# In the last feed-forward block of a three-block network, GpSimd issues each gather only once the preceding one has landed

## The reference

```python
def ffn(x):                       # x is the layer-normed activation, 4096 x 256
    p = sigmoid(x @ gate_w.T); p = p / p.sum(-1)
    w, idx = top_k(p, 2)          # two of 16 experts for each token
    w = w / w.sum(-1)
    gate, up = split(x @ gate_up_proj[e])      # 256 -> 2 * 128, for each expert e
    y = (silu(gate) * up) @ down_proj[e]       # 128 -> 256
    return sum over the two chosen experts of w * y
x = x + 0.5 * ffn(layernorm(x))
x = x + attention(layernorm(x))   # 16 heads of 16, causal
x = x + 0.5 * ffn(layernorm(x))
```

## Time and profile before

| | us |
|---|---|
| median of 3 runs | 785.37 |
| fastest, slowest of them | 782.91, 786.13 |
| profiled execution, first to last instruction (its span) | 862.8 |
| in it: last block, first gather issued | 593.05 |
| in it: last expert tile copied out of PSUM | 810.55 |
| in it: first and last gather behind the last store | 813.29 and 853.55 |

### The profile page before, as it was taken

The page is one execution under the profiler, slowest core; times in us unless marked ns, Lnnn a source line. Parts: engine busy times, 40 slices in busy tenths (PEclk is TensorE's granted clock), DMA queues, the critical chain, the costliest instruction groups (busy, mean ns, idle before and its releaser), DMA issues. The chain is left out here.

```text
span 862.8 us, 17915 instructions
## 1 busy us (share of the span) xinstructions
PE 666.8 (77%) x5486; PEld 538.4 (62%) x5503; DVE 520.5 (60%) x1407; ACT 403.7 (47%) x962; POOL 397.6 (46%) x466
## 2 busy tenths in 40 slices
PE   2649999978699999999999998674553999777300
PEld 1438888867367777777777776453342999666300
DVE  7887533426588888888988875378511344244333
ACT  2534666644155555556655654571112666443100
POOL 4134555555445544444554322403375554346274
PEclk9859999989699999999999999985665999889655
DMA  7873555545544434444343330051243567334453
GB/s 244 284 244 108 159 162 161 162 126 143 155 133 128 129 113 117 117 127 124 112 112 107 103 102 27 3 196 44 66 116 95 156 162 149 101 101 137 138 178 118
DMA packets 94160, 113.48 MB, mean 132 GB/s; under 512 B 11648, under 2 KB 84624, under 8 KB 94096
## 3 DMA queue, kind: packets, MB, share of 16 engines
q1 hardware_dynamic: 80240, 74.87, 27.5%
q0 software_dynamic: 13824, 37.77, 17.4%
q10 hardware_dynamic: 32, 0.02, 0.0%
HBM read 49.30 MB, written 33.55 MB: 96 GB/s over the span
## 5 line engine op out<-in xcount | busy, mean ns | idle before, releaser
L876 PE MATMUL bank<-xeT,shared 128*128 128x128 f32 x1280 | 181.2, 288 | 14.3 <-ACT xeT L992 9.1
L704 POOL DMA_INDIRECT spare<-normed,source x128 | 123.0, 961 | 140.2 <-PE bank L867 57.0
L876 PEld LDWEIGHTS bank<-xeT,shared 128*128 128x128 f32 x1280 | 166.6, 203 | 17.6 <-issue 17.3
L1142 DVE TENSOR_TENSOR hid<-bank,silu 128x128 f32<-128x128 f32 x160 | 46.6, 291 | 184.1 <-ACT silu L996 109.1
L370 POOL TENSOR_SCALAR_AFFINE_SELECT pr<-pr 128x512 f32<-128x512 f32 x128 | 81.0, 655 | 156.3 <-ACT pr L537 155.9
L883 PE MATMUL bank<-wd_sb,hid 128*128 x320 | 107.4, 419 | 47.7 <-issue 28.2
L594 DVE TENSOR_REDUCE mx<-bank 128x2 f32<-128x512 f32 (+1 forms) x192 | 127.9, 687 | 23.5 <-PE bank L443 20.9
L537 ACT ACTIVATE pr<-bank 128x512 f32<-128x512 f32 x192 | 102.8, 609 | 32.1 <-PE bank L465 19.6
L1006 ACT COPY shared<-wgu_sb 128x512 f32 x160 | 97.9, 613 | 26.0 <-DVE eid L1163 16.1
L996 ACT ACTIVATE silu<-bank 128x128 f32<-128x128 f32 x160 | 44.6, 279 | 136.6 <-PE bank L876 82.2
L715 POOL DMA_INDIRECT shared<-grouped_out,slot x64 | 62.8, 981 | 65.6 <-DVE x_sb L1316 25.1
(11 more groups left out here) (175 smaller groups left out, 1051.3 us busy)
## 6 DMA issues: line engine op xcount, KB each, us to landing
grouped_out<-shared SPq DMA_DIRECT2D x160, 128.0 KB
shared<-parts SPq DMA_DIRECT2D x154, 128.0 KB
spare<-parts SPq DMA_DIRECT2D x70, 128.0 KB
normed<-shared SPq DMA_DIRECT2D x16, 512.0 KB, 3.6
wgu_sb<-_L_ffn_gate_up_proj_dram SPq DMA_DIRECT2D x8, 512.0 KB, 8.7
out_dram<-x_sb SPq DMA_DIRECT2D x16, 256.0 KB
x_sb<-in_L_attn_x_dram SPq DMA_DIRECT2D x3, 1024.0 KB, 10.1
wd_sb<-in_L_ffn_down_proj_dram SPq DMA_DIRECT2D x4, 512.0 KB, 8.9
```

Of the source, the lines that this page charges most:

```text
L704: nc.gpsimd.indirect_dma_start(xe[f][r], None, normed, bass.IndirectOffsetOnAxis(source[:, j:j + 1], 0)).then_inc(arrival(f, r), 16)
L876: last = nc.tensor.matmul(bank[2 + u][:, h * P:(h + 1) * P], wgu_tile[u][:, c, h * I:(h + 1) * I], xeT[:, u, c, :], start=(c == 0), stop=( ...
```

## The change

Two helper functions name the count that the semaphore of a gather has when that gather has landed: `row_landed(j)` for the rows of expert tile j and `result_landed(t, j)` for result j of token tile t. In the last block (f is 1 there and 0 in the first one) `fetch(j)` waits for `row_landed(j - 1)` from j = 1 on. `fetch_results` waits before each gather for the one before it, apart from the very first of the results (token tile 0, result 0), which does not wait for the last row gather. No instruction is moved, no other engine's code is touched, and no buffer changes. The number of gathers stays 144; 142 of them get the wait.

```diff
+            def row_landed(j):
+                r = j % AHEAD[f]
+                pool.wait_ge(arrival(f, r), arrived(f, r, j // AHEAD[f]) + 16 * (r % 2 + 1))
+
+            def result_landed(t, j):
+                pool.wait_ge(at[f"gathered{t % LATE}"], 16 * TOPK * (NT // RING + t // LATE) + 16 * (j + 1))
+
             def fetch(j):
 
                 r = j % AHEAD[f]
                 if j >= AHEAD[f]:
                     pool.wait_ge(s["xe_transposed"], j - AHEAD[f] + 1)
+                if f and j:
+                    row_landed(j - 1)
                 nc.gpsimd.indirect_dma_start(xe[f][r], None, normed, ...
@@
                 if t >= LATE:
                     pool.wait_ge(s["x_done"], t - LATE + 1)
                 for j in range(TOPK):
+                    if t or j:
+                        result_landed(t if j else t - 1, 1 - j)
                     nc.gpsimd.indirect_dma_start(late[:, t % LATE, j, :], None, grouped_out, ...
```

## The result

The changed kernel takes 1089.18 us (median of 4 runs, 1088.92 to 1091.23) where the kernel before takes 785.31 (4 runs). The ratio is 1.385, 95% interval 1.381 to 1.389. The forecast was 1034 us with a range up to 1070: the sign and most of the size were right, and the time lies outside the range.

What follows compares the result with a forecast made beforehand. Expert tiles set the pace until the last gather train; the waits would make GpSimd's gathers the chain, 141 steps of 3.1 us. Span +182.6 us, plus 66 us of stops absent from timed runs, on 785.4: 1034 us, range 1000 to 1070.

Steps and rivals of the forecast that it cites:

- the turn: Between the two halves of the result gathers: last landing, two combine operations, copy of tile 79 and its store, 7.2 us.
- 66 us of stops: Last block of the profiled kernel before: compute-engine stops and the slower clock behind them, taken as absent from timed runs.
- the 77.4 us: Excess of the profiled execution's span, 862.8 us, over the median of the runs, 785.4 us, for the kernel before.
- The rival with the stops in the timed runs: Last block's engine stops also occur in timed runs, so the spans' difference of 182.6 us applies: 968 us, chance 0.15.
- c: Last block, start to start of gathers on GpSimd with the new wait: 3.1 us in place of 1.26, bounds 2.85 to 3.4.
- Row steps: Row gathers of the last block's expert tiles: 79 steps of 3.1 us, 244.9 us.
- the first half of the results: Result gathers of the first 16 token tiles: 31 steps of 3.1 us, 96.1 us.
- the second half: Result gathers of the last 16 token tiles: 31 steps of 3.1 us, 96.1 us.
- the end: After the last result gather: its landing, two combine operations and the output store, 6.8 us.
- that rival (949 us): Last block: a gather alone lands sooner than with two or three under way, c 2.5 us, time 949 us, chance 0.07.
- The 2.3 us: The skill page's estimate for c: fixed 2.0 us plus bytes / 436e3 for 131072 bytes; sum lower by 113 us.
- The faster rival: Last block: waits break up the gather trains that stop other engines, returning 66 us; needs c of 1.8 us, chance 0.02.

Runs made afterwards that it cites:

- the second profile: The kernel before, unchanged, profiled once more: its span is 788.3 us, where the first profile's was 862.8 us.
- the small-store kernel: The changed kernel with the stores of the last block's expert tiles cut to the first 32 of 256 columns: 1092.5 us.
- two and up to four gathers under way: Against the changed kernel, waits before every second gather only: for the pair before it, 930.5 and 917.7 us; for the pair before that, 868.1 and 792.5 us.
- the kernel with the landing wait first: The changed kernel with each gather's two waits in the other order, landing ahead of the buffer or x_done wait: 1047.8 us, and 1047.4 in the second series.
- the kernel that would tell: The kernel before with a 128x256 memset before each row gather and first-half result gather of the last block, no landing waits: 805.1 and 807.2 us.

## Why the prediction was right and wrong

**The bound and the chain were right.** GpSimd's gathers became one chain through the last block. The 17th gather came 51 us after the first (forecast about 50), the wait for the second routing was hidden, the turn took 6.9 us (7.2), the experts stood still from tile 61 on, and the two halves of the change, run apart, added up to the whole within 4 us. One part of the reading of the kernel before holds for its profile alone: GpSimd is ahead of everybody until 797 us there, while in the second profile it sets the pace from about 709 us on.

**From the span to the time: right.** The prediction took 66 us of stops for something that the timed runs do not have. The second profile of the kernel before has none of them and 154 us for the experts of the last block. The other 11 of the 77.4 us were to lie ahead of the block, and the first gather goes out at 583.19 us in that profile, and at 581.38 in the changed kernel, in place of 593.05. The whole change in time is 303.9 us; the forecast of 248.6 plus the error of the chain (below, 53.3) is 301.9. The rival with the stops in the timed runs (968 us) is out for these runs. But it is no fiction: beside three of the experiments the kernel before did take 865 us, over 13 runs. An estimate from its 864.7 us, the 1092.5 us of the small-store kernel beside it and the 6 to 7 us that small stores save is that the change would cost 225 to 235 us there and not 304; it was not run there as it is. That the timed runs have no stops was thus true of those that were timed first, and not of all.

**What failed is one term: c, the step from gather to gather.** It was put at 3.1 us with an upper bound of 3.4; the mean over the 141 steps is (278.9 + 106.2 + 103.6) / 141 = 3.47. Row steps cost 34.0 us more than the forecast, the first half of the results 10.1, the second half 7.5, the end 2.1, the turn 0.3 less, together 53.3 us. The reading of the earlier trace rows was sound: 3.0 to 3.1 us is what a gather with one wait over 128 different rows takes in most steps (1.66 us to the first packet, 0.75 of packets, 0.60 to the next start). Two things were left out of it.

- A second wait. The prediction said of the waits for buffers and for `x_done` that they are met, and costed them at nothing. Met or not, they took the place in the gather instruction, and the landing wait became an instruction of its own, with 0.45 us behind it. 48 row gathers and 27 result gathers have two waits, beside the first one of the turn. Put in the other order they give back 41 us.
- What is fetched. The rows of a gather are not the same work if they are the same row. Fourteen steps behind gathers of tiles with few or no tokens took up to 0.85 us longer; those without tokens gave back 4.5 us when given other row numbers. In the kernel with the landing wait first the 14 steps take 52.2 us, 9 to 10 more than 14 others of its row steps (3.08 us each).

The two sum to 50 to 51 us, against 51.6 of the steps alone. The upper bound was set by traffic, and traffic was a small matter: with stores of 16 KB in place of 128 KB the chain is 6 to 7 us shorter, 0.05 us a step, and the long steps stay. Nor does the bound follow from its own words: a seventh of the way from 3.1 to 4.7 us is 3.33, and at c = 3.4 the prediction's sum gives 1076 us and not 1070. The measured time lies outside either.

**A gather alone does not land sooner.** The shortest steps measured were 2.9 us from issue to issue, so the forecast was right not to go below its rows, and that rival (949 us) is out. The small spread of the four landings says nothing on what part of them is fixed, as all four gathers have the same size; the packets do, with 0.75 of 3.0 us. The 2.3 us worked out from the Trainium skill, "DMA: Bandwidth & Descriptors", section "Anatomy of one DMA — SWDGE (gpsimd) path", are not borne out as a step from gather to gather.

**The faster rival** needed c below 1.8 us, and c was 3.47. Even with two gathers under way the steps (2.2 us on average) stay above that limit.

**What stays open** is why the longer executions are longer. In the four profiles of that kind (the kernel before, small stores, two and up to four gathers under way) the first gather of the last block goes out at 590.8 to 594.6 us, and in the others at 580 to 584: some 10 us are lost before any gather of the block is issued. The rest lies in the stops of all compute engines. They come with trains at 1.26 us and up to four gathers under way, and the one profile of that kind with two under way has none. Whether it is the pace or the number was not separated, since the kernel that would tell ran only where there were no stops. What the engines wait for is not shown.

## What to carry to other kernels

Before a wait is put on a queue of transfers, price the chain that it makes: its length in steps times the whole way from issue to issue, not to landing, and look for the depth at which it costs next to nothing (here four gathers under way: 7 us, two: 132, one: 262 to 304 by the order of the waits). If an instruction has two waits, put first in the code the one that will be met last, as the first one went into the gather here, and read on the timeline whether the pauses fall into kinds. Before an experiment counts as no gain, compare the stretch that it was to change and not the time alone. A profile whose span is far from the median of the runs is of another case than the runs, and a second one costs little.

## What was not expected of the hardware

- A gather on GpSimd that carries its landing wait itself starts 2.0 us after the end of the one before it; with the landing wait as a separate instruction 2.5 us.
- A gather of 128 times the same 1 KB row of HBM pauses the chain for 3.3 us where one of 128 different rows pauses it for 2.5; its packets take 1.6 us in place of 0.75.
- The same kernel took 785 us in four series of runs and 865 in a fifth. A profile shows some 10 us of the difference ahead of the block's first gather and the rest in stops of three engines during trains of gathers. The one kernel with a single gather under way that stands beside the 865 us (small stores) lost only the 10 us.
